# Products of the last layer inside the meetings of the second, turned outputs ahead of a unit, the stream's first logits behind the output projection

## The reference, cut to what matters

```python
# layer 0: attention with 16 heads of 16, x + tanh(gate) * out
# layer 1: RWKV block: token shift, low-rank mix, r, k, v, g, decay w; then over the tokens
#   out = r . (u * k v^T + s);  s = k v^T + w * s        (s: 8 x 8 for each of 32 heads)
#   y = group_norm(out) * silu(g);  x = x + y @ Wo.T;  then the channel mix (fk, fr, fv)
# layer 2: attention with 32 heads of 8 and grouped keys, then layernorm
# layer 3, for each of two attentions:
q = layernorm(x) @ wq + bq                      # 16 heads of 128
k, v = ctx @ wk + bk, ctx @ wv + bv             # from the context alone
x = x + softmax(q k^T / sqrt(128)) v @ wo + bo  # with one bias row of keys and values
# and x = x + gelu(layernorm(x) @ w_fc1 + b1) @ w_fc2 + b2
```

## Time and profile before

| | us |
|---|---|
| time, median of 3 executions (1239.31 to 1241.22) | 1240.67 |
| time of the profiled execution | 1239.29 |
| span of the profiled execution | 1237.5 |
| layer 0, to PE's last product of it | 0 to 144.4 |
| layer 1, four batches | 145.8 to some 415 |
| layer 2 | some 415 to 650 |
| layer 3's attentions | 650 to 1173.7 |
| MLP | 1175.6 to 1237.5 |

### The profile page before, as it was taken

One profiled execution on the slowest core, in us unless ns is written; L12 is line 12 of the kernel. 1 busy time (PEld: TensorE's weight loads), 2 busy tenths in 40 slices (PEclk: granted clock), 3 DMA queues, 4 the chain that ended last, 5 costly groups with the idle time before them and its releaser, 6 DMA issues.

```text
span 1237.5 us, 17677 instructions
## 1 busy us (share of the span) xinstructions
PE 1183.3 (96%) x5936; PEld 835.9 (68%) x5936; DVE 792.6 (64%) x2357; ACT 536.9 (43%) x1233; POOL 215.6 (17%) x430
## 2 busy tenths in 40 slices
PE   6898899999998999999989999999999999999998
PEld 4576555555555444444337888888888888888787
DVE  4755386877766778778655666666656666667520
ACT  3465434454445355555553444343333343433332
POOL 3241252425153120301011000000000000000000
PEclk8999999999999899999999999999999999999999
DMA  8777211111118545244349040404030211400000
GB/s 247 182 195 233 88 66 69 52 60 56 56 60 228 176 147 167 90 150 138 111 148 369 3 137 1 136 1 137 1 114 24 89 49 64 142 1 2 1 9 26
DMA packets 95033, 124.42 MB, mean 101 GB/s; under 512 B 7264, under 2 KB 72960, under 8 KB 92704
## 3 DMA queue, kind: packets, MB, share of 16 engines
q1 hardware_dynamic: 94320, 123.00, 30.9%
q10 hardware_dynamic: 624, 0.30, 0.1%
HBM read 79.33 MB, written 43.65 MB: 99 GB/s over the span
## 4 chain that ended last, share of the span: by engine, by line
PE 87%; DVE 4%; ACT 3%; issue 2%; POOL 2%; DMA 2%; ACTq 1%; SPq 0%; POOLq 0%; DVEq 0%
PE J L2589 9%; PE J L2567 9%; PE TT L2577 9%; PE OO L1117 5%; PE OO L1120 5%; PE S L2534 5%; PE TT L2551 5%; PE OO L2534 4%; PE J L1120 3%; PE J L1389 2%; PE J L329 2%; PE OO L2814 2%; PE S L1361 2%; PE J L1117 2%; PE TT L329 2%
## 5 line engine op out<-in xcount | busy, mean ns | idle before, releaser
L2646 ACT ACTIVATE PT<-TT 128x512 f32<-128x512 f32 x128 | 76.4, 597 | 280.5 <-PE TT L2551 280.5
L2685 POOL COPY On<-probs 128x8 f32<-128x8 f32 x128 | 29.0, 227 | 471.0 <-DVE probs L2720 441.8
L2731 DVE TENSOR_SCALAR QK<-J,cols 128x256 f32<-128x256 f32 x126 | 61.0, 484 | 67.8 <-PE J L2567 67.8
L2720 DVE TENSOR_SCALAR probs<-probs,inv 128x257 f32<-128x257 f32 x256 | 79.0, 352 | 4.5
L2551 PE MATMUL TT<-ident,probs 128*128 128x128 f32 x512 | 77.0, 273 | 2.3 <-DVE probs L2720 2.3
L1120 PE MATMUL OO<-ctxT,weights_a 128*128 128x512 f32 x144 | 70.2, 610 | 5.8 <-SPq L313 3.3
L2551 PEld LDWEIGHTS TT<-ident,probs 128*128 128x128 f32 x512 | 63.7, 141 | 16.4 <-DVE probs L2720 3.7
L2726 DVE COPY km<-TT 128x256 f32<-128x256 f32 x128 | 54.2, 423 | 30.3 <-PE TT L2577 30.0
L2414 DVE TENSOR_TENSOR_SCAN early<-km,early 128x256 f32<-128x256 f32 x64 | 64.3, 1045 | 10.9 <-ACT early L2172 10.1
L1117 PE MATMUL OO<-weights_a,ctxT 128*128 128x512 f32 x136 | 67.8, 622 | 3.4 <-SPq L313 2.9
L2589 PE MATMUL J<-early,km 128*128 128x256 f32 x256 | 65.8, 379 | 0.3 <-DVE km L2726 0.3
(11 more groups left out here) (423 smaller groups left out, 2619.7 us busy)
## 6 DMA issues: line engine op xcount, KB each, us to landing
wide_keys<-weights_a SPq DMA_DIRECT2D x43, 256.0 KB, 2.1
wide_values<-weights_a SPq DMA_DIRECT2D x40, 256.0 KB, 2.0
weights_a<-wide_keys SPq DMA_DIRECT2D x16, 512.0 KB, 7.2
weights_a<-wide_values SPq DMA_DIRECT2D x16, 512.0 KB, 8.5
early<-wide_keys SPq DMA_DIRECT2D x16, 512.0 KB, 8.4
early<-wide_values SPq DMA_DIRECT2D x16, 512.0 KB, 9.2
query_parts<-weights_a SPq DMA_DIRECT2D x32, 192.0 KB, 2.8
weights_a<-in_L_xattn_wv SPq DMA_DIRECT2D x2, 2048.0 KB, 8.9
```

Source lines behind the costliest of these rows:

```text
L2646: act.activation(PT[:, n % 2, :], T0[:, :], ACT.Copy).then_inc(pt3_ready, 1)
L2720: ins = dve.tensor_scalar(P_[n % 2][:, qt, :], P_[n % 2][:, qt, :], inv[:, qt, n % 32:n % 32 + 1], None, ALU.mult)
```

## The change

Units go to the batches as 15, 13, 13, 15 instead of 13, 13, 13, 17. Unit 8 is computed in layer 0's tail, in two halves around `flip_od`, and copied by ACT before the meeting. Units 9 (bank S1) and 10 (O1) are issued by PE after it has arrived at the first meeting and before it waits for `go`; ACT copies both at the start of batch 0. `OPENING` counts those three units, and `SCAN0` is the number of the unit in O1. In the meetings between batches PE waits for `gvar_ready`, arrives, and then issues late unit 4 and the next batch's opening unit before it waits for `go`; ACT copies late unit 4 behind the meeting, and SP stores it behind `lead`. PE waits for the copies ahead of the mix products. At `j` = 7 come `front_pe`, `gather(3)`, the second half of the seventh scan unit (its first half is at `j` = 6) and `turn_y(1)`, now ahead of late unit 0. The last product into `read` is DVE's instead of POOL's. ACT keeps the last outputs ahead of the seventh unit's copy. The last batch has seven late units instead of nine. At the stream's start the logits of item 0 come behind the output projection, and ACT's copy of the bias rows behind its first exponents. Before the MLP PE arrives at the meeting, then issues 9 of the 16 products of `widen` (three of four for the banks J0, S0 and S1) and only then waits for `go`; the rest follow behind it.

```diff
@@ -799,10 +799,17 @@
                 pe.wait_ge(ot0_ready, STEPS0 - 1)
+                pe.wait_ge(loaded["ahead"], 16)
+                project_ahead(pe, S0, UNIT0[0], range(1))
                 flip_od(STEPS0 - 1)
+                project_ahead(pe, S0, UNIT0[0], range(1, KC))
...
                 project_out(B - 1)
-                meet(pe, "pe")
+                pe.drain().then_inc(arrived, 1)
+                project_ahead(pe, S1, UNIT0[0] + 1)
+                project_ahead(pe, O1, UNIT0[0] + 2)
+                pe.wait_ge(go["pe"], 1)
+                pe.sem_clear(go["pe"])
@@ -907,6 +914,7 @@
                 fetch_on(STEPS0 - 1)
+                copy_ahead(act, S0, UNIT0[0])
@@ -1086,11 +1094,13 @@

-        EACH = [13, 13, 13, 17]
+        EACH = [15, 13, 13, 15]
         UNIT0 = [FIRST + sum(EACH[:b]) for b in range(B)]
+        OPENING = [3, 1, 1, 1]
+        SCAN0 = [UNIT0[b] + OPENING[b] - 1 for b in range(B)]
         IN_SCAN = DIM1 - 1
-        LATE0 = UNIT0[B - 1] + 1 + IN_SCAN
-        LATE = EACH[B - 1] - 1 - IN_SCAN
+        LATE0 = SCAN0[B - 1] + 1 + IN_SCAN
+        LATE = EACH[B - 1] - OPENING[B - 1] - IN_SCAN
@@ -1106,12 +1116,12 @@

-        def project_ahead(pe, bank_, u):
+        def project_ahead(pe, bank_, u, steps=range(KC)):
...
                 pe.wait_ge(loaded["ahead_k1"], 16)
-            for k in range(KC):
+            for k in steps:
@@ -1119,7 +1129,8 @@
                                    ctxT[:, k, pair * 512:pair * 512 + 512], start=(k == 0), stop=(k == KC - 1))
-            mm.then_inc(ahead_done, 1)
+            if KC - 1 in steps:
+                mm.then_inc(ahead_done, 1)
@@ -1526,11 +1537,11 @@
                     flip_od(STEPS2 - 1, T0)
-                    logits = slots3["pe"](pe)
-                    logits(0)
...
                     project_out(B - 1, J1)
+                    logits = slots3["pe"](pe)
+                    logits(0)
@@ -1603,8 +1614,6 @@
                     fetch_on(STEPS2 - 1, T1)
-                    act.wait_ge(ahead_stored[2], stores_before(2 * UNITS, 2))
-                    bias_rows_act(act, 0, T1)
@@ -1868,18 +1877,20 @@

+            LAST_LATE = EACH[0] - OPENING[0] - IN_SCAN - 1
+
...

-            def runs(eng, name, main):
+            def runs(eng, main, meeting):
...
                 main(0, None, 1, 1)
-                meet(eng, name)
+                meeting(0)
...
                     main(b, b - 1, 1, b + 1)
-                    meet(eng, name)
+                    meeting(b)
@@ -1915,21 +1926,21 @@

+                def ahead_late(b, n):
+                    u0 = SCAN0[b]
+                    u = u0 + 1 + IN_SCAN + n
+                    if b < B - 1 and n in (2, 3):
+                        pe.wait_ge(ahead_copied, u0 + 1 + IN_SCAN)
+                        pe.wait_ge(kv_ready, DIM1)
+                    elif b < B - 1 and n >= 4:
+                        pe.wait_ge(ahead_copied, u - 3)
+                    elif n >= 2:
+                        pe.wait_ge(ahead_copied, u - 1)
+                    project_ahead(pe, late_bank(b, n), u)
+
                 def main(b, b_before, following, b_next):
-                    u0 = UNIT0[b]
-
-                    def ahead_late(n):
-                        u = u0 + 1 + IN_SCAN + n
-                        if b < B - 1 and n in (2, 3):
-                            pe.wait_ge(ahead_copied, u0 + 1 + IN_SCAN)
-                            pe.wait_ge(kv_ready, DIM1)
-                        elif b < B - 1 and n >= 4:
-                            pe.wait_ge(ahead_copied, u - 3)
-                        elif n >= 2:
-                            pe.wait_ge(ahead_copied, u - 1)
-                        project_ahead(pe, late_bank(b, n), u)
-
-                    project_ahead(pe, O1, u0)
+                    u0 = SCAN0[b]
+
@@ -1943,6 +1954,7 @@
                     pe.wait_ge(lora_ready, 1)
+                    pe.wait_ge(ahead_copied, u0)
@@ -2027,8 +2039,13 @@
                             mm.then_inc(bonus_done, 1)
+                        if j == DIM1 - 1:
+                            pe.wait_ge(v_ready, 1)
+                            front_pe(following, pe, S1, None)
...
                             gather(j // 2)
+                        if j == DIM1 - 1:
+                            project_ahead(pe, J0, u0 + j, range(1, KC))
@@ -2040,18 +2057,15 @@
                                 project_fv(1)
-                        if j == 5:
-                            pe.wait_ge(v_ready, 1)
-                            front_pe(following, pe, S1, None)
...
                         if j < IN_SCAN:
-                            project_ahead(pe, J0, u0 + 1 + j)
+                            project_ahead(pe, J0, u0 + 1 + j, range(KC) if j < IN_SCAN - 1 else range(1))
+                    turn_y(1, O1)
                     pe.wait_ge(bonus_ready, 1)
-                    ahead_late(0)
-                    turn_y(1, O1)
+                    ahead_late(b, 0)
...
@@ -2079,16 +2093,22 @@
                         slot(-9)
-                        ahead_late(6)
+                        ahead_late(b, 6)
                         slot(-8)
-                        ahead_late(7)
                         slot(-7)
-                        ahead_late(8)
                     else:
-                        for n in range(1, EACH[b] - 1 - IN_SCAN):
-                            ahead_late(n)
-
-                runs(pe, "pe", main)
+                        for n in range(1, LAST_LATE):
+                            ahead_late(b, n)
+
+                def meeting(b):
+                    pe.wait_ge(gvar_ready, 1)
+                    pe.drain().then_inc(arrived, 1)
+                    ahead_late(b, LAST_LATE)
+                    project_ahead(pe, O1, UNIT0[b + 1])
+                    pe.wait_ge(go["pe"], 1)
+                    pe.sem_clear(go["pe"])
+
+                runs(pe, main, meeting)
@@ -2124,12 +2144,17 @@

+                def copy_late(b, n):
+                    copy_ahead(act, late_bank(b, n), SCAN0[b] + 1 + IN_SCAN + n)
+
                 def main(b, b_before, following, b_next):
-                    u0 = UNIT0[b]
+                    u0 = SCAN0[b]
...
                     def late(n):
-                        copy_ahead(act, late_bank(b, n), u0 + 1 + IN_SCAN + n)
-
+                        copy_late(b, n)
+
+                    if b_before is None:
+                        copy_ahead(act, S1, u0 - 1)
@@ -2195,8 +2220,8 @@
                                 fetch_fv(1)
+                    keep_y(1)
                     copy_ahead(act, J0, u0 + 7)
-                    keep_y(1)
@@ -2230,14 +2255,16 @@
                         slot(-8)
-                        late(7)
                         slot(-7)
-                        late(8)
                     else:
-                        for n in range(2, EACH[b] - 1 - IN_SCAN):
+                        for n in range(2, LAST_LATE):
...

-                runs(act, "act", main)
+                def meeting(b):
+                    meet(act, "act")
+                    copy_late(b, LAST_LATE)
+
+                runs(act, main, meeting)
@@ -2280,7 +2307,7 @@
                     pool.wait_ge(r_ready, 1)
-                    for j in range(DIM1):
+                    for j in range(DIM1 - 1):
...
@@ -2417,6 +2444,11 @@
                             times_k(j + 1)
+                    dve.wait_ge(state_ready, DIM1)
+                    dve.wait_ge(read_ready, DIM1 - 1)
+                    dve.wait_ge(y_done, (DIM1 - 5) // 2 + 1)
+                    dve.tensor_tensor(read[(DIM1 - 1) % 4], rT, state[(DIM1 - 1) % 2][:, :, 0:S], ALU.mult)\
+                        .then_inc(read_ready, 1)
...
@@ -2626,7 +2658,14 @@
                 add_bias_rows(GROUPS3 - 1)
-                meet(pe, "pe")
+                pe.wait_ge(h3_ready, GROUPS3)
+                pe.wait_ge(exp3_ready, ITEMS3)
+                pe.drain().then_inc(arrived, 1)
+                pe.wait_ge(loaded["fc"], 16 * 2)
+                for i in WIDENED:
+                    widen_first(pe, i)
+                pe.wait_ge(go["pe"], 1)
+                pe.sem_clear(go["pe"])
@@ -2654,6 +2693,8 @@
                 exponents(0)
+                act.wait_ge(ahead_stored[2], stores_before(2 * UNITS, 2))
+                bias_rows_act(act, 0, T1)
@@ -2786,6 +2827,14 @@

+        WIDENED = (0, 2, 3)
+
+        def widen_first(pe, i):
+            for n in range(2 * KC - 1):
+                o, k = n // KC, n % KC
+                pe.matmul((J0, J1, S0, S1)[i][:, o * S:(o + 1) * S], fc1[:, k, (2 * i + o) * P:(2 * i + o + 1) * P],
+                          hT[:, k, 0:S], start=(k == 0), stop=(k == KC - 1))
+
@@ -2822,9 +2871,16 @@

-                pe.wait_ge(loaded["fc"], 16 * 2)
+                def widen_last(i):
+                    k = KC - 1
+                    pe.matmul(banks[i][:, S:2 * S], fc1[:, k, (2 * i + 1) * P:(2 * i + 2) * P],
```

(13 more changed lines are left out.)

10 lines of the change are left out of this document (5 added, 5 removed).

## The result

The changed kernel takes 1242.35 us (median of 20 executions, 1239.13 to 1245.06) against 1239.11 us before (20 executions): ratio 1.0032 [1.0023, 1.0041], slower by 0.3%. The forecast was 1238.4 us, 2.3 us faster than before. The profiled execution's span is 1240.3 us, 2.8 more than before.

The account below looks back on a forecast made before the run. PE, busy 96% of the span, was taken as the bound, with time won where it waits on the chain. +10.5 - 1.2 - 1.7 - 1.4 - 5.3 - 3.2 = -2.3 us gave 1238.4 us, range 1231.5 to 1243.5.

Parts of the forecast that it names:

- A: Layer 0's tail and batch 0's head: loses 10.5 us, unit 8's store behind two loads delaying ACT's tanh, then low clock.
- B: Outputs turned ahead of a unit, last read on DVE: gains 1.2 us, 0.4 in each of batches 1 to 3.
- C: Products inside the three meetings between batches: fill PE's wait for the release, gaining 1.7 us, capped by DVE's end.
- D: Two units fewer in batch 3's tail: gains 1.4 us, two of DVE's waits before stacked slots go.
- E: The stream's start: PE works during its waits of 3.18 and 1.27 us, so the turn comes 5.3 us earlier.
- F: The MLP's start: nine products replace the wait of 1.93 us and the clock stays full, gaining 3.2 us.
- my slower rival: Rival 3: batch 0's head stays at 1.2 GHz after the idle, 1244.2 us; chance 13%.
- the cap: In B: DVE's last product still ends at 199.22, as the root needs ACT's Sqrt behind a table load of 1.28.
- Rival 2: The meetings give all: DVE's end moves with its earlier start, C is 4.9 us, total 1235.2; chance 13%.
- Rival 1: Unit 8's store doesn't hold ACT, landing in 2.0 to 2.6 us; A is 0.1, total 1228.0; chance 5%.
- Rival 3: Batch 0's head stays at 1.2 GHz for 16 us, losing 8 instead of 2.2, total 1244.2; chance 13%.

Follow-up runs that it names:

- no meeting work: Kernel with both repairs, but PE issues nothing inside the three meetings between batches, as in the kernel before: 1231.44 us, ratio to before 0.9945.
- old units: Changed kernel with POOL's tail held and units given out as before (13, 13, 13, 17; none in layer 0's tail): 1231.55 us, ratio to before 0.9935.
- both repairs: Changed kernel with unit 8's store ahead of the two loads and POOL's two channel-mix products held until DVE's last product: 1228.70 us, ratio to before 0.9932.
- tail held: Changed kernel, but POOL waits for DVE's last product into read before its two channel-mix products: 1239.22 us, ratio to before 1.0006.

## Why the prediction was wrong

The sum said -2.3 us and the time moved by +3.2 (by the profiled spans +2.8). The terms as measured, from the table and, for the head, the tail of layer 0 (last weighing to batch 0's start: 8.76 before, 9.23 after):

| part | forecast | measured | from |
|---|---|---|---|
| A | +10.5 | +11.2 | 0.47 + 10.72 |
| B | -1.2 | 0.0 | +0.33, +0.03 and +0.14 in the periods (no meeting work against before), -0.54 in batch 3 (old units against before) |
| C | -1.7 | -1.5 | no meeting work against both repairs |
| POOL beside DVE | 0 | +3.6 | tail held against after |
| D | -1.4 | -1.1 | old units against both repairs |
| layer 2 | 0 | -0.8 | 227.32 to 226.56 |
| E | -5.3 | -5.1 | 13.44 to 8.38 |
| F | -3.2 | -3.1 | 13.82 to 10.74 |

With the 0.4 by which layer 0 was shorter in the profile of after, that is the 2.8 us of the spans, 5.1 more than the forecast. Part B's -0.54 and some 0.5 of layer 2's 0.8 are one stretch at the low clock: the last unit ahead of the first slot took 3.76 before and 3.12 with the old units, the slot's own products 1.06 and 0.60.

- **The step that failed** is in part B, "With that read on DVE": the move of one instruction from POOL to DVE was put at nothing, and what POOL would do with the time it got was not asked. It starts its next two products at once, beside DVE's last scans and the moved product: 2.80 and 1.58 instead of 1.84 and 0.69. That cost 3.6 us, over two thirds of the whole error of 5.1. The rows to see it by were in the trace (scan pairs of 2.60 with POOL's products beside them, 1.84 with the end of one read, 1.39 with nothing), and my slower rival should have been this and not the clock.
- **Part A** was right in mechanism and place: the store behind the two loads held ACT for 10.67 us, as the earlier trace rows let one work out. The wait was 8.91, 0.4 under the forecast (8.6 and the 0.73 that was there). The term too small was the clock: 7.5 us at 0.59 cost 2.9, where I took 2.2 from stretches of 3.4 and 3.9 us. Layer 0's tail cost 0.5 rather than 0.1. The estimate from the Trainium skill, "DMA: Bandwidth & Descriptors", section "Anatomy of one DMA", was 2.6 us for this store; the section gives its sum as a fit for DMAs that GpSimd issues, which I had not said, and this store is issued by SyncE. Where the store stands first it took at most 2.3, near that estimate, and behind 3 MB 10.8.
- **Part B** beside the failed step: the 0.4 a batch never came. The stretch of the earlier trace rows took 8.42 in batch 1 with the tail held, against 8.37 before and a forecast of 7.9 to 8.1. Nor would it have counted: PE has slack up to the meeting, and the period is DVE's loop, by way of the turn and ACT's root. There I had misread a wait. I wrote that DVE waited for the root already; before, that wait was 0.32 us (254.74), and DVE stood for the second turn. With the turn ahead the wait for the root became 2.11, so the cap held all the same.
- **Part C** was right (1.5 for 1.7): DVE's end caps it, and the root behind the copy of late unit 1 and its table load is the cap. Rival 2 (4.9 us) fell: 1.5.
- **Part D, E and F** were right within 0.3 each. In E no transfer was late.
- **Rival 1** (the store isn't held) fell by the 10.67 us. **Rival 3** (the head stays at 1.2 GHz for 16 us) fell too: 7.5 us, 2.9 lost, where it decided from 7.

The time stayed inside the range (1231.5 to 1243.5), but not by the mechanism: slower had 0.19, of it 0.13 for a clock that stays low, and what made the kernel slower stood in no rival. Layer 2's 0.8 the other way, which no term had, was luck.

Apart from the store's place and POOL's early products, the parts of the change do no harm or gain. With the store issued ahead of the loads, POOL's tail held and the root ahead of one copy it takes 1226 us (medians 1226.22 and 1225.95; 0.9905 [0.9888, 0.9922] and 0.9891 [0.9868, 0.9914]), 12 to 13 us under the kernel before, where the change as made lost 3.

## What to carry to other kernels

- Where an instruction moves from one engine to another, ask what the engine that is relieved does in the time it gains. An instruction of POOL that reads SBUF next to DVE's scans or two-input products is a cost to DVE; look in the trace for the same DVE instruction at two durations, and what ran beside it.
- A room that is reused sooner turns its store into a wait; the store's price is then set by what stands ahead of it in the issuing queue. Issue the small store that somebody waits for ahead of the large loads that nobody needs yet.
- Waits removed from an engine with slack are no gain. Find the loop that sets the period first (here DVE, by way of ACT's root), and where two things hold one engine in the same place, expect their removal to pay only together.

## What the hardware showed that I had not expected

- DVE's pair of scans (128x256) took 1.39 us with nothing of POOL beside it, 1.84 with the end of one read of POOL beside its first half (1.83 with memsets beside the rest), 2.14 with copies, 2.60 to 2.80 with two-input products; a two-input product of DVE (128x512) 0.69 alone or beside memsets, 0.92 and 1.58. POOL is slowed as well: its products 1.27 alone, 1.53 and 1.66 beside DVE, its copies 0.61 and 1.01. By the ends of the rows the two take turns by the whole instruction.
- One 256 KB store let its waiter go 2.3 us after its issue ahead of 3 MB of loads, and 10.8 behind them, on the same queue.
- After 8.9 us without work the granted clock was 0.50 for the first 6 us and 0.59 over 7.5. After a wait of 2.02 us it fell in some executions (a unit of 2.92 to 3.50 us) and not in others (1.88), and so it did after waits of 0.81, 0.81 and 0.47 us in layer 0's tail.
